# Second graph layer: source scores of tiles 5 to 9 from their input rows, and the first aggregated tile prepared below the last products

## The reference, cut to what matters

```python
def _gat_layer(x, W, a_src, a_dst, b, src, dst, n_nodes):
    h = x @ W
    e_src = h @ a_src
    e_dst = h @ a_dst
    e = leaky_relu(e_src[src] + e_dst[dst], 0.2)
    m = segment_max(e, dst)
    w = exp(e - m[dst])
    z = segment_sum(w, dst)
    alpha = w / z[dst]
    out = segment_sum(h[src] * alpha[:, None], dst)
    return out + b
h = relu(_gat_layer(x, W1, att_src1, att_dst1, b1, src, dst, 1250))
out = _gat_layer(h, W2, att_src2, att_dst2, b2, src, dst, 1250)
```

## Time and profile before

| | us |
|---|---|
| median of three runs (lowest, highest) | 1493.97 (1488.02, 1497.21) |
| the profiled execution | 1489.21 |
| its span, from the first to the last instruction | 1487.5 |
| PE busy in it | 1375.7 |
| DVE busy | 1126.6 |
| ACT busy | 914.1 |

### The profile page before, as it was taken

One profiled execution on the slowest core, in us unless ns is written; L12 is line 12 of the kernel. 1 busy time (PEld: TensorE's weight loads), 2 busy tenths in 40 slices (PEclk: granted clock), 3 DMA queues, 4 the chain that ended last, 5 costly groups with the idle time before them and its releaser, 6 DMA issues.

```text
span 1487.5 us, 25322 instructions
## 1 busy us (share of the span) xinstructions
PE 1375.7 (92%) x8889; PEld 1319.7 (89%) x8889; DVE 1126.6 (76%) x1543; ACT 914.1 (61%) x1601; POOL 436.6 (29%) x335
## 2 busy tenths in 40 slices
PE   2996999899799999899999999999998997799997
PEld 2995988899699999799999999999997997699997
DVE  5888998635889653586868868778688887788885
ACT  6887777322467322447847568486687421699995
POOL 1000000000000010335636446265476400355553
PEclk9997999999899999999999999999999998799999
DMA  7001000221334620000000000000011596376651
GB/s 202 8 1 42 16 25 23 71 92 38 105 94 145 195 86 0 22 1 2 21 1 21 0 0 21 0 21 0 0 32 40 154 294 146 118 169 166 162 103 26
DMA packets 48640, 99.17 MB, mean 67 GB/s; under 512 B 7178, under 2 KB 23182, under 8 KB 48554
## 3 DMA queue, kind: packets, MB, share of 16 engines
q1 hardware_dynamic: 40787, 75.04, 16.2%
q0 software_dynamic: 7488, 22.26, 7.5%
q10 hardware_dynamic: 279, 0.77, 0.2%
HBM read 67.23 MB, written 33.70 MB: 68 GB/s over the span
## 4 chain that ended last, share of the span: by engine, by line
PE 65%; DVE 6%; issue 3%; ACT 2%; DMA 2%; POOL 1%; ACTq 0%; POOLq 0%; SPq 0%; DVEq 0%
PE ps L421 13%; PE ps L422 13%; PE ps L423 13%; PE ps L912 5%; PE ps L957 4%; PE ps L959 4%; PE ps L958 3%; PE ps L936 3%; PE ps L938 3%; DVE mcol L1181 1%; POOL prlo L1144 1%; PE ps L1370 1%; PE ps L661 1%; DVE prlo L1144 1%; ACT prob L1082 1%
## 5 line engine op out<-in xcount | busy, mean ns | idle before, releaser
L1144 POOL TENSOR_TENSOR prlo<-prob,prhi 125x500 fp32r<-125x500 f32 x180 | 257.0, 1434 | 250.1 <-ACT prob L1082 249.2
L1181 DVE TENSOR_REDUCE mcol<-ps 125x1 f32<-125x1250 f32 x120 | 175.0, 1459 | 76.2 <-PE ps L912 74.1
L1080 ACT ACTIVATE prhi<-ps 125x500 fp32r<-125x500 f32 x300 | 176.8, 589 | 72.0 <-PE ps L938 65.3
L957 PE MATMUL ps<-prhi,vhi 125*128 125x250 f32 x600 | 171.6, 286 | 10.4 <-POOL prlo L1144 6.9
L1082 ACT ACTIVATE prob<-ps 125x500 f32<-125x500 f32 x300 | 176.1, 587 | 0.7 <-DVE prlo L1144 0.6
L959 PE MATMUL ps<-prlo,vhi 125*128 125x250 f32 x600 | 168.0, 280 | 0.0
L958 PE MATMUL ps<-prhi,vlo 125*64 125x250 f32 x600 | 167.0, 278 | 0.0
L936 PE MATMUL ps<-qst,kst 128*125 128x250 f32 x600 | 155.7, 283 | 2.7 <-ACT val L614 1.1
L421 PE MATMUL ps<-hhi,pthi 125*125 125x384 f32 x400 | 155.0, 388 | 3.0 <-DVE ptlo L784 3.0
L938 PE MATMUL ps<-q,k 128*125 128x250 f32 x600 | 153.4, 280 | 0.0
L1666 POOL MEMSET q<- 128x2500 f32 x1 | 2.2, 2185 | 503.3 <-PE ps L423 503.3
(11 more groups left out here) (343 smaller groups left out, 3849.7 us busy)
## 6 DMA issues: line engine op xcount, KB each, us to landing
w1all<-in_L_ffn_W_dram SPq DMA_DIRECT2D x8, 1152.0 KB, 9.0
w2st<-in_L_ffn_W_dram SPq DMA_DIRECT2D x8, 1152.0 KB
wqst<-in_L_ffn_Wqkv_dram SPq DMA_DIRECT2D x12, 384.0 KB, 4.2
hid_d<-tin SPq DMA_DIRECT2D x10, 375.0 KB
hin<-hid_d SPq DMA_DIRECT2D x10, 375.0 KB
vtin<-xn_d SPq DMA_DIRECT2D x10, 375.0 KB
out_dram<-accr POOLq DMA_DIRECT2D x10, 375.0 KB, 8.3
xres<-in_x_dram SPq DMA_DIRECT2D x10, 336.0 KB
```

The costliest lines, as they stand in the source:

```text
L957: pe.matmul(ps[:, b:b + GQ], vhi[:, e, kt, :], hi, start=kt == 0, stop=False)
L1080: act.activation(prhi[:, n % RING, :], bank(3 + n % 3, P, 2 * GQ), ACT.Exp, scale=float(HD) ** -0.5)
L1144: eng.tensor_tensor(prlo[:, n % RING, :], prob[:, n % 3, :], prhi[:, n % RING, :].bitcast(f32), ALU.subtract)\
L1181: dve.tensor_reduce(mcol[:, e, t:t + 1], ps[0:P, 0:N], AX.X, ALU.max, negate=True).then_inc(sem("max"), 1)
```

## The change

- `W2 a_src` is computed on DVE, one dot product for each of the six pieces of W2 (`product_score2`, 128 partitions by 768), written to DRAM as 768 single elements (`wa_d`) and read back broadcast to 125 partitions (`wab`).
- For tiles 5 to 9 the source score is no longer taken from the product in PSUM; it is the dot product of the reloaded row tile, with its negatives set to zero, and `wab` (`row_score2`), done three tiles ahead. Tiles 0 to 4 keep their score from the product.
- `es` goes to DRAM element by element and comes back as a broadcast row `esb`, in two parts: tiles 0 to 7 (1000 columns) and tiles 8 and 9 (250). The diagonals, their matmuls and the copies from PSUM are gone; `es02` is made from `esb` on ACT.
- The maximum, leaky sum, exponential and weighing of the first aggregated tile move into the products of tiles 7 and 8; its `turned` stands ahead of the last product, and its `higher` ahead of the last `result2`. `lower`, the maximum and `leaky` of tile 1 follow below the last product.
- The two row buffers lie apart: `hin0` is on space that is free once the last counts are unpacked, `hin1` on the slots of `wst`. `row_in(0)` moves ahead of the last four weight loads on SP; `row_in(9)` now stands between the two broadcasts.
- The steps at which the six pieces of W2 are split are set one by one.

```diff
...
+ROWS_FROM, EARLY_ES = 5, 8 * P
...
 def weight2_at(k):
-    return max(turn_at(7, 17) + 7 * k, STEPS + 1 + 7 * k)
+    return (turn_at(7, 17), turn_at(8, 1), turn_at(8, 10), turn_at(8, 13), turn_at(8, 17), turn_at(8, 19))[k]
+def weight2_low_at(k):
+    return (turn_at(7, 20), turn_at(8, 4), turn_at(8, 11), turn_at(8, 16), turn_at(8, 18), turn_at(8, 20))[k]
...
+    wac = put("wac", [128, KD], f32)
...
-    hin = put("hin", [P, 2, D], f32, at=WSTAT)
+    hin0 = put("hin0", [P, D], f32, at=OHDG)
+    assert put.end <= top[0]
+    hin1 = put("hin1", [P, D], f32, at=WSTAT)
+    wab = lg2[:, 1, 0:D]
...
-                if t == T - 1 and h == 1:
-                    nine2_pe(pe)
...
+                else:
+                    pe.wait_ge(sem("tile_lo"), 2 * T + 2)
+                    turned(pe, 1, 0, 0)
                 product2(pe, t)
...
-            if t == T - 1:
-                act.wait_ge(sem("scored"), 4 * T - 1)
...
+        def sloped2(act, a, b, n):
+            act.wait_ge(sem("agg_l"), T)
+            act.wait_ge(sem("src_moved"), 32 * n + 32)
+            act.activation(es02[:, a:b], esb[:, a:b], ACT.Copy, scale=SLOPE).then_inc(sem("agg_sl"), 1)
         def linear2_act(act, between):
             for t in range(T):
                 if t + 1 < T:
                     higher2(act, t + 1)
-                if t < T - 1:
-                    result2(act, t)
+                if t == 6:
+                    sloped2(act, 0, EARLY_ES, 1)
+                if t == T - 2:
+                    exponential(act, 1, 0)
+                if t == T - 1:
+                    higher(act, 1, 0)
+                result2(act, t)
+                if t == 7:
+                    sloped2(act, EARLY_ES, N, 2)
                 between(t)
...
+        def scores2(t, a):
+            return 2 * T + (2 * t + a if t < ROWS_FROM else ROWS_FROM + t)
...
+            dve.wait_ge(sem("tile_yhi"), T + t + 1)
+            dve.wait_ge(sem("scored"), scores2(t, a))
+            if t == ROWS_FROM:
                 dve.wait_ge(sem("g1_out1"), 16 * (T // 2))
-            dve.scalar_tensor_tensor(halves(tin[:, 1, :] if late else esb[:, 0:D]), two(4 + 2 * (t % 2), P, HALF), 1.0,
-                                     halves(att[:, a, :]), ALU.mult, ALU.mult, accum_out=(es, ed)[a][:, t:t + 1])\
+            dve.scalar_tensor_tensor(halves(esb[:, 0:D] if t < ROWS_FROM else tin[:, 1, :]), two(4 + 2 * (t % 2), P, HALF), 1.0,
+                                     halves(att[0:P, a, :]), ALU.mult, ALU.mult, accum_out=(es, ed)[a][:, t:t + 1])\
                 .then_inc(sem("scored"), 1)
...
+        def product_score2(dve, k):
+            if k == 0:
+                dve.wait_ge(sem("att_in"), 64)
+            dve.wait_ge(sem("w_hi"), KD + k + 1)
+            dve.wait_ge(sem("src_parts"), k)
+            dve.scalar_tensor_tensor(wjunk[:, :], wst[:, k % 2, :], 1.0, att[:, 0, :], ALU.mult, ALU.mult,
+                                     accum_out=wac[:, k:k + 1]).then_inc(sem("src_parts"), 1)
+        def row_score2(dve, t):
+            n = t - ROWS_FROM
+            if n == 0:
+                dve.wait_ge(sem("src_moved"), 32)
+                dve.wait_ge(sem("g1_out0"), 16 * (T // 2))
+            dve.wait_ge(sem(f"tile_in{t % 2}"), 16 * (t // 2 + 1))
+            dve.wait_ge(sem("src_parts"), KD + n)
+            dve.scalar_tensor_tensor(tin[:, 0, :], hin(t)[:, :], 0.0, wab, ALU.max, ALU.mult,
+                                     accum_out=es[:, t:t + 1]).then_inc(sem("src_parts"), 1)
...
-        def nine2_pe(pe):
-            pe.wait_ge(sem("agg_diag"), 3)
-            for b, c in ((0, 500), (1, 500), (2, 125)):
-                last = pe.matmul(bank(b, P, c), ones[:, 0:P], diag1[:, 500 * b:500 * b + c], start=True, stop=True)
-            last.then_inc(sem("agg_esb_raw"), 1)
-        def last2_pe(pe):
-            pe.wait_ge(sem("agg_diag"), 4)
-            pe.matmul(bank(3, P, 125), ones[:, 0:P], diag1[:, NINTH:N], start=True, stop=True)\
-                .then_inc(sem("agg_esb_raw"), 1)
-        def nine2_act(act):
-            act.wait_ge(sem("agg_esb_raw"), 3)
-            act.activation(halves(esb[:, 0:1000]), two(0, P, 500), ACT.Copy).then_inc(sem("agg_esb"), 1)
-            act.activation(esb[:, 1000:NINTH], bank(2, P, 125), ACT.Copy).then_inc(sem("agg_esb"), 1)
-        def last2_act(act):
-            act.wait_ge(sem("agg_esb_raw"), 4)
-            act.activation(esb[:, NINTH:N], bank(3, P, 125), ACT.Copy).then_inc(sem("agg_esb"), 1)
         def linear2_dve(dve, order):
             for t in range(T - 1):
-                lower2(dve, t + 1)
-                score2(dve, t, 0)
-                if t == T - 2:
-                    slopes2(dve, order, 0, T - 2)
-                    diagonal2(dve, 0, T - 1)
+                if t == 7:
+                    lower2(dve, t + 1)
+                    dve.wait_ge(sem("far_ready"), T + 1)
+                    dve.wait_ge(sem("src_moved"), 64)
+                    far_part(dve, order, 0, EARLY_ES, 6)
+                    dve.wait_ge(sem("agg_raw"), T + 1)
+                    dve.wait_ge(sem("agg_sl"), 3)
+                    leaky_part(dve, 0, EARLY_ES)
+                elif t == T - 2:
+                    dve.wait_ge(sem("src_moved"), 96)
+                    far_part(dve, order, EARLY_ES, N, 7)
+                    order.wait()
+                    order.did(dve.tensor_tensor(zsum[:, 0, 2:3], zsum[:, 0, 6:7], zsum[:, 0, 7:8], ALU.max))
+                    shift_sum(dve, order, 1, 0)
+                    shift(dve, order, 1, 0)
+                    dve.wait_ge(sem("agg_sl"), 4)
+                    leaky_part(dve, EARLY_ES, N).then_inc(sem("agg_l"), 1)
+                    lower2(dve, t + 1)
+                    weigh(dve, 1, 0)
+                else:
+                    lower2(dve, t + 1)
+                if ROWS_FROM <= t + 3 < T:
+                    row_score2(dve, t + 3)
+                if t < ROWS_FROM:
+                    score2(dve, t, 0)
                 score2(dve, t, 1)
                 rest2(dve, t)
+                if t == ROWS_FROM:
+                    slopes2(dve, order, 0, ROWS_FROM)
...
-            turned(pe, n, 0, 0)
-            sums(0, 0, range(T))
+            pe.wait_ge(sem("tile_yfree"), T * (n + 1) + 1)
+            sums(0, 0, range(T - 1))
+            pe.wait_ge(sem("tile_yfree"), T * (n + 1) + 2)
+            sums(0, 0, range(T - 1, T))
             turned(pe, n, 1, 1)
             sums(0, 0, range(T, 2 * T))
+            pe.wait_ge(sem("scored"), 2 * T + 2 * ROWS_FROM + T - ROWS_FROM)
...
-            nine2_act(act)
-            nine_sloped(act, 0)
-            result2(act, T - 1)
-            last2_act(act)
-            last_sloped(act, 3)
-            exponential(act, n, 0)
...
-            dve.wait_ge(sem("far_ready"), T + 1)
-            dve.wait_ge(sem("agg_esb"), 5)
-            far_part(dve, order, 0, NINTH, 6)
-            score2(dve, T - 1, 0)
-            diagonal2(dve, T - 1, T)
-            dve.wait_ge(sem("agg_sl"), 3)
-            leaky_part(dve, 0, NINTH)
-            dve.wait_ge(sem("agg_esb"), 6)
-            far_part(dve, order, NINTH, N, 7)
-            order.wait()
-            order.did(dve.tensor_tensor(zsum[:, 0, 2:3], zsum[:, 0, 6:7], zsum[:, 0, 7:8], ALU.max))
-            shift_sum(dve, order, n, 0)
-            shift(dve, order, n, 0)
-            dve.wait_ge(sem("agg_sl"), 4)
-            leaky_part(dve, NINTH, N).then_inc(sem("agg_l"), 1)
+            lower(dve, n, 0)
+            maximum(1)
+            leaky(dve, n, 1)
             rest2(dve, T - 1)
-            weigh(dve, n, 0)
-            maximum(1)
-            dve.wait_ge(sem("agg_w"), T * n + 1)
-            lower(dve, n, 0)
-            leaky(dve, n, 1)
             score2(dve, T - 1, 1)
-            slopes2(dve, order, T - 2, T)
+            slopes2(dve, order, ROWS_FROM, T)
             maximum(2)
...
                     sp.wait_ge(sem("w_lo"), KD + k - 1)
+                    sp.wait_ge(sem("src_parts"), k - 1)
...
             def row_in(t):
-                if t < 2:
+                if t == 0:
+                    sp.wait_ge(sem("cnt_ready"), T)
+                elif t == 1:
                     sp.wait_ge(sem("w_lo"), 2 * KD)
+                    sp.wait_ge(sem("src_parts"), KD)
                 else:
                     sp.wait_ge(sem("tile_raw"), T + t + 1)
+                if t >= ROWS_FROM + 2:
+                    sp.wait_ge(sem("src_parts"), KD + t - ROWS_FROM - 1)
                 sp.wait_ge(sem(f"g1_out{t % 2}"), 16 * (t // 2 + 1))
-                sp.dma_start(hin[:, t % 2, :], hid_d[t * P:(t + 1) * P, :]).then_inc(sem(f"tile_in{t % 2}"), 16)
+                sp.dma_start(hin(t)[:, :], hid_d[t * P:(t + 1) * P, :]).then_inc(sem(f"tile_in{t % 2}"), 16)
             weights2(0)
             weights2(1)
             for t in range(7):
                 row_out(t)
+            row_in(0)
             for k in range(2, KD):
                 weights2(k)
             row_out(7)
```

(52 more changed lines are left out.)

21 lines of the change are left out of this document (7 added, 14 removed).

## The result

The changed kernel takes **1497.61 us** (median of 20 runs, 1492.91 to 1503.41); the kernel before, measured beside it, takes 1492.57 (20 runs). The ratio is 1.0041, 95% interval 1.0031 to 1.0050: 0.4% slower, where 1.4% faster was forecast. The profiled execution took 1502.39, its span is 1500.7.

What follows compares the result with a forecast made beforehand. PE was taken as the bound (65% of the chain), with time won where it stands or runs slowly. Savings of 6.2 + 14.2 = 20.4 us gave a forecast of 1473.6, rounded to 1473, range 1466 to 1487.

Steps and rivals of the forecast that it cites:

- Part A: End of the first layer: earlier weighing of tile 9 and earlier row tile 0 save 6.2 us, bounds 5.1 to 7.2.
- part B: Border to the aggregation: second `turned` starts 14.2 us after product 8 instead of 28.4, saving 14.2.
- DVE's chain: At the border, DVE's gapless work from row tile 9 landing to the first `turned`: 12.0 us.
- The list beside part B: Border saving itemised: 2.2 broadcast matmuls, 10.4 standing, 2.2 low clock, less the two new waits.
- The lead: Behind the border, DVE stays ahead of PE through `turned` of tile 2, with nothing to spare.
- R3: Aggregation: DVE loses its lead, 4 to 6 us given back over tiles 1 to 3; time 1479; chance 0.10.
- Step 1: Border: the store of 1000 elements takes 1.3 us and 0.4 to complete.
- The prediction's other end of 6: Border: element store at 6 us, by 512-byte packets of a weight load; saving then 9.5.
- R1: Border: dearer element stores make the first `turned` 4.7 to 10 us late; time 1478 to 1484; chance 0.15.
- Step 2: SP's queue behind row tile 1: eight 125-row transfers at 3.1 us each from 298.5 on.
- a stall of 1.0: At `transposes2(5)`, waiting on `lower2(4)` behind late row tile 5: 1.0 us, bounds none and 2.1.
- R2: Queue behind row tile 1 bounds: `transposes2` 1, 4, 5 wait, 2 to 4 us saved there; time 1477; chance 0.11.

Runs made afterwards that it cites:

- run 7: Run 6 with row tile 1 loaded a piece earlier, the W2 a store behind it and the bias behind row tile 5: 1471.97 us, ratio 0.9872.
- run 3: Changed kernel with ScalarE increments, scores stored as rows of 32 and 8 bytes, attention weights not the reference's: 1478.96 us, ratio 0.9918.
- run 5: Changed kernel, ScalarE program length as in run 1, scores stored as rows and put in node order by ScalarE copies: 1479.82 us, ratio 0.9925.
- run 1: Changed kernel with four semaphore increments nobody waits for added to ScalarE ahead of the attention loop: 1489.02 us, ratio 0.9983.
- run 6: Run 5 with W2 a also stored as rows, 24 bytes a partition, read at that stride: 1477.54 us, ratio 0.9904.
- run 4: Run 1 with the second layer's bias load moved behind row tile 5: 1486.52 us, ratio 0.9958.

## Why the prediction was wrong

**Where it was right.** The changed kernel and run 7 have `turned` of tile 9 with 0.54 and 0.56 idle (under 1 forecast) and `transposes2(0)` with none. Run 7 has `transposes2(1)` at 302.49 (302.9), the clock at 1.00, 20.4 us saved at the second `turned` (20.4), and 18 to 19 us of the time (ratio 0.9872). That the 20.4 is met to the tenth is luck. Part A gives 7.6 there (358.79 before, 351.17 now, at tile 8), part B 12.8 (42.2 from there to the second `turned` before, 29.4 now), for 6.2 and 14.2: an error of 1.4 each way. DVE's chain took 14.1 instead of 12.0 and row tile 9 landed 2.3 earlier than forecast, 1.4 of them by part A. Part B by itself is met in run 3, which stores rows and leaves the columns unordered: 28.0 from tile 8, as forecast (42.2 less 14.2). The list beside part B in the prediction (2.2, 10.4 and 2.2, less the two waits of 0.45 and 1.0) adds up to 13.3 and not to 14.2; it leaves out that the first `turned` took 2.46 before instead of 1.1. The forecast itself goes by the other sum. The lead is kept behind the border (R3 didn't come: 11.6 from one `turned` to the next). But run 7 isn't the change; three steps of the prediction failed on it.

**Step 1, the completion of the element stores** ("by it 1.3, and 0.4 to complete"). The 1.3 held: the packets went in 1.4. The 0.4, for which the prediction gave no row, is 4.1, and 5.2 for the 250 elements; in these stretches the views show no packet of the stores. From issue to completion that is 8.1 instead of 4.2, and 6.4 instead of 2.5 for the second store. The prediction's other end of 6 put the doubt in the packets, where it wasn't. As rows the two take 2.8 and 2.9 from issue to issue, of which 0.5 and 2.0 lie behind the last packet (run 3). From tile 8 to the second `turned` the forecast was 28.0 and the changed kernel took 37.9. The 9.9 between them are 4.0 of the first store, 0.9 until row tile 9 is there, 3.3 of the second store (DVE's wait of 3.37 for the second broadcast) and 1.7 from the first `turned` to the second, by the low clock. That is rival R1, chance 0.15, in size too: the first `turned` came at 383.12, 8 us late beside the 8.0 of part A (R1: 4.7 to 10), but R1 laid it to the packets. Its measured share is the 9 to 10 us by which runs 5 and 3 are under run 1. The Trainium skill, "DMA: Bandwidth & Descriptors", section Rules for kernel authors, says to rearrange such an access, and runs 3 and 5 agree with the advice. By the page's 10.5 ns a packet, in section Bandwidth, the estimate was 10.5 us for the 1000 elements and would be 2.6 for the 250; measured are 1.4 ns a packet and a completion that hardly depends on their number.

**Step 2, the queue behind row tile 1** ("at 3.1 each from 298.5 on"; a stall of 1.0). I listed eight transfers of 125 rows and left the store of W2 a out, though it stands among them and is the same kind as the one that I priced for part B. It delays row tile 1 by 2.2 and those behind it (run 6), and the eight transfers make `transposes2(4)` wait beside it (runs 4 and 6). Without the element store, in run 6, `transposes2(4)` still waits for row tile 4 until 326.6 where it was forecast to land at 323.6: 3.5 a transfer instead of 3.1, over the 3.3 that the prediction named as a sign of being wrong. At tile 8 part A lost 1.8 (358.79 before, 360.58 after) where 6.2 saved were forecast: 8.0 missing. This is R2, chance 0.11, and worse than its 2 to 4 saved; its condition was named as an alternative to R1, and both held. Of the 20.4, 8.0 are missing by the queue and 9.9 by the border behind tile 8; 2.5 are left. The waits had the low clock behind them, which I had counted where a wait went and not where one came.

**Step 3, what I hadn't looked for.** The prediction followed what the change does to data, queues and engines, and not what it does to the length of a program ahead of a loop. With steps 1 and 2 alone the kernel would be 0.2% faster (run 1), inside the 1% of no change; the four increments fewer on ScalarE make it 0.4% slower than before. No rival had this. That the time lies within 1% of before had a chance of 0.27, but given for R1 or part of R3 alone; what came is R1, R2 and the loop together. The trace of before showed that ScalarE's instruction queue fetches little in the loop, so the question could have been put, but not which way two instructions fewer would turn it.

**Open.** Why a store of elements is reported 4 to 5 us after its last packet isn't shown; that it is the size of the pieces is (runs 3 and 5). That ScalarE's gaps in the loop are waits for the extra fetches is argued from their coming and going together; what is shown is that the place of the loop brings both. In the two profiled executions with slow turns the last scatter of the experts also lies 4 us farther behind the first than in the others (187 us instead of 183); whether that belongs to the loop's state or to those executions (both are above their kernel's median) can't be told from one profile each.

## What to carry to other kernels

Price a small store by how it is cut and by its completion, not by its bytes or packets alone: put the elements of a partition side by side, and let the reader pay for the order where an engine has time. When a transfer is added to a full queue, walk the whole queue with it, since two small delays on it add up and a wait can also cost clock behind it. After any edit compare the length of the turns of each hardware loop with before; if an untouched loop has slowed, count the instructions ahead of it on each engine and the fetches of each instruction queue before looking for another cause.

## What the runs showed of the hardware

- A store of 1000 elements of 4 bytes from SBUF to DRAM takes 7.8 to 8.1 us from issue to the next dependent issue, one of 250 elements 6.3 to 6.4 (changed kernel, runs 1 and 4); 4.1 and 5.2 of it lie behind the last packet. The same bytes in pieces of 32 and 8 bytes take 2.8 to 3.1 (runs 3 and 5 to 7).
- A transfer issued 0.3 us before such a store (768 elements) on the same queue lands some 2 us later than when these are stored in pieces of 24 bytes (runs 5 and 6).
- A loop's turns are 94.5 us or up to 99.0 us long, by four instructions of ScalarE more or fewer ahead of it, with 2 or 16 fetches of 8 KB over three turns (run 1 and the changed kernel).
- Strided reads of 4-byte elements: on DVE 1.6 to 1.7 us instead of 0.96 for 768 columns at a stride of 24 bytes, on ScalarE 2.2 instead of 1.04 for 1000 columns at 32 bytes, but 0.43 instead of 0.41 for 250 columns at 8 bytes (run 7).
- A wait put down to "issue" can be a real wait: 2.56 at `transposes2(1)` went when its load came sooner, and the 2.03 and 1.53 at the first `turned` end where DVE's `weigh` ends (383.0 and 366.6).
